# A conditioned residual block on one core: VectorE's last two lags of the convolution by quarters, the second pair of sums inside the variance's wait, short products of constants on TensorE, and the second spread one tile later

## The reference, cut to what matters

```
x = x + conv(x, cond)          # depthwise, causal: at position t, channel c the sum over lags j = 0..31
                               # of cond[31 - j, c] * x[b, t - j, c], nothing from before the sequence
ada = cond @ ada_w + ada_b     # shift1, scale1, gate1, shift2, scale2, gate2, one row for each sequence
x1 = ln(x) * (1 + scale1) + shift1      # ln: (x - mean) * (var + 1e-6) ** -0.5 over the 256 channels
q, k, v = split(x1 @ qkv_w + qkv_b)     # 16 heads of 128
y = x + gate1 * (softmax(q k^T / sqrt(128)) v @ out_w + out_b)
x2 = ln(y) * (1 + scale2) + shift2
y = y + gate2 * (gelu(x2 @ ffn_w1 + ffn_b1) @ ffn_w2 + ffn_b2)
out = x + y                    # x here with the convolution in it
```

## Time and profile before

| | |
|---|---|
| median of three runs | 312.05 us (311.78 to 312.29) |
| profiled execution, its own time | 311.19 us |
| span of its instructions | 309.4 us |
| granted TensorE clock over the span | 1.0 of full speed (2.4 GHz) |
| TensorE busy | 300.4 us (97%) |
| VectorE busy | 179.6 us (58%) |
| ScalarE busy | 174.6 us (56%) |
| GpSimd busy | 119.7 us (39%) |

### The profile page before, as it was taken

The page is one execution under the profiler, slowest core; times in us unless marked ns, Lnnn a source line. Parts: engine busy times, 40 slices in busy tenths (PEclk is TensorE's granted clock), DMA queues, the critical chain, the costliest instruction groups (busy, mean ns, idle before and its releaser), DMA issues.

```text
span 309.4 us, 6184 instructions
## 1 busy us (share of the span) xinstructions
PE 300.4 (97%) x2614; PEld 253.6 (82%) x2614; DVE 179.6 (58%) x311; ACT 174.6 (56%) x317; POOL 119.7 (39%) x104
## 2 busy tenths in 40 slices
PE   7989899999999999989999999999999999999995
PEld 7876797888898888878888888888898888878885
DVE  3996697987866648471446674350720455757232
ACT  5943368434762755466367636644763693824901
POOL 5215818331911543163327134630915471311500
PEclk9999999999999999999999999999999999999999
DMA  7902421500160061007002400520090000000022
GB/s 240 376 5 69 125 81 46 162 0 2 41 232 0 4 218 55 0 4 271 1 4 102 169 2 2 174 100 0 14 330 0 2 0 3 0 1 2 0 68 68
DMA packets 15275, 23.00 MB, mean 74 GB/s; under 512 B 808, under 2 KB 8336, under 8 KB 15248
## 3 DMA queue, kind: packets, MB, share of 16 engines
q1 hardware_dynamic: 15200, 22.58, 21.7%
q10 hardware_dynamic: 48, 0.03, 0.0%
HBM read 21.57 MB, written 1.05 MB: 73 GB/s over the span
## 4 chain that ended last, share of the span: by engine, by line
PE 86%; DVE 8%; POOL 2%; ACT 2%; issue 1%; DVEq 0%; POOLq 0%
PE bank L1025 16%; PE bank L1027 16%; PE bank L1026 16%; PE bank L1112 9%; DVE xc L592 5%; PE bank L1033 5%; PE bank L1034 4%; PE bank L1035 4%; PE bank L1096 3%; PE bank L1235 2%; PE bank L1237 2%; PE bank L1236 2%; POOL wl L309 1%; PE bank L964 1%; PE bank L1004 1%
## 5 line engine op out<-in xcount | busy, mean ns | idle before, releaser
L309 POOL TENSOR_TENSOR wl<-raw,wh 128x512 fp32r<-128x512 f32 x70 | 94.3, 1373 | 123.2 <-ACT wh L382 105.3
L433 ACT ACTIVATE pool<-bank,bT 128x512 f32<-128x512 f32 x56 | 38.5, 687 | 52.6 <-PE bank L1027 52.6
L1025 PE MATMUL bank<-x1h,wl 128*128 128x512 f32 (+1 forms) x174 | 65.7, 377 | 0.1
L1026 PE MATMUL bank<-x1l,wh 128*128 128x512 f32 (+1 forms) x174 | 64.6, 371 | 0.0
L1027 PE MATMUL bank<-x1h,wh 128*128 128x512 f32 (+1 forms) x174 | 64.6, 371 | 0.0
L732 DVE SCALAR_TENSOR_TENSOR ol<-bank,bT,oh 128x512 fp32r<-128x512 f32 x32 | 24.0, 750 | 34.0 <-ACT oh L458 33.0
L592 DVE SCALAR_TENSOR_TENSOR xc<-x,condT,xc 128x496 f32<-128x496 f32 (+27 forms) x80 | 42.1, 598 | 0.1
L382 ACT ACTIVATE wh<-raw 128x512 fp32r<-128x512 f32 x70 | 39.8, 622 | 0.0
L1025 PEld LDWEIGHTS bank<-x1h,wl 128*128 128x128 f32 x174 | 32.8, 189 | 6.3 <-POOL wl L309 0.5
L1027 PEld LDWEIGHTS bank<-x1h,wh 128*128 128x128 f32 x174 | 32.8, 188 | 5.7
L1026 PEld LDWEIGHTS bank<-x1l,wh 128*128 128x128 f32 x174 | 32.8, 188 | 5.3
(11 more groups left out here) (146 smaller groups left out, 433.4 us busy)
## 6 DMA issues: line engine op xcount, KB each, us to landing
raw<-in_L_cond_qkv_w_dram SPq DMA_DIRECT2D x24, 512.0 KB, 5.3
raw<-in_L_cond_out_w_dram SPq DMA_DIRECT2D x8, 512.0 KB, 3.6
raw<-in_L_cond_ffn_w_dram SPq DMA_DIRECT2D x3, 512.0 KB, 6.1
adaw<-in_L_cond_ada_w_dram SPq DMA_DIRECT2D x1, 1024.0 KB, 9.8
out_dram<-pool SPq DMA_DIRECT2D x3, 256.0 KB, 2.2
xtok<-in_x_dram SPq DMA_DIRECT2D x2, 256.0 KB, 3.2
adaw<-in_L_cond_ada_w_dram SPq DMA_DIRECT2D x1, 512.0 KB, 4.7
xtok<-in_x_dram SPq DMA_DIRECT2D x1, 512.0 KB, 5.7
```

The costliest lines, as they stand in the source:

```text
L309: g.tensor_tensor(wl[:, cols], raw[:, cols], wh[:, cols].bitcast(F32), ALU.subtract)\
L433: a.activation((q_sb if j < GH else k_sb)[:, j % GH, :], src, ACT.Identity, bias=bias(U, j // GH, j % GH)).then_inc(s_ev, 1)
L1025: pe.matmul(dst, wl[:, w_cols], a_hi, start=start, stop=False)
L1026: pe.matmul(dst, wh[:, w_cols], a_lo, start=False, stop=False)
```

## The change

There are four edits, all in the first 36 us.

1. VectorE's lags 11 and 12 of the first half (`END_LAGS`) are taken out of `conv(0, ...)` and made by quarters in a new function `conv_end(n)`, each with half the elements and twice as many instructions; `conv_sum(n)` waits for the end of `conv_end(n)` through a semaphore of its own.
2. The order on VectorE becomes: `conv_end(0)`, `conv_sum(0)`, `conv_end(1)`, `modulation(0)`, `centre(0)`, `one_plus`, `scale_up(0)`, `var_eps(0)`, and only then `conv_sum(1)`.
3. TensorE makes eight products of constants (32 columns of weights, 64 columns moving, into a bank that nobody reads then) before `mean(0)`.
4. `spread(1)` on TensorE stands behind tile 2 of the first quarter's projections instead of behind tile 1.

```diff
+    END_LAGS = DVE_LAGS[0][-2:]
+    STEPS_BEFORE = [0, CT * (len(DVE_LAGS[0]) - len(END_LAGS))]
...
+            def conv_end(n):
+                for i, j in enumerate(END_LAGS):
+                    for ct in range(CT):
+                        xs = by_batch(part(x0, ct, CHUNKS[n]))
+                        acc = by_batch(part(xc, ct, CHUNKS[n]))[:, :, j:]
+                        if i:
+                            v.wait_ge(s_cend[n], CT * (i - 1) + ct + 1)
+                        else:
+                            v.wait_ge(s_cdve, STEPS_BEFORE[1] - CT + ct + 1)
+                        v.scalar_tensor_tensor(out=acc, in0=xs[:, :, :T - j], scalar=condT[:, ct, T - 1 - j:T - j],
+                                               in1=acc, op0=ALU.mult, op1=ALU.add).then_inc(s_cend[n], 1)
+
             def conv_sum(n):
-                v.wait_ge(s_cdve, STEPS_BEFORE[1])
+                v.wait_ge(s_cend[n], CT * len(END_LAGS))
...
-            conv(0, 0, len(DVE_LAGS[0]))
+            conv(0, 0, len(DVE_LAGS[0]) - len(END_LAGS))
+            conv_end(0)
             conv_sum(0)
-            conv_sum(1)
+            conv_end(1)
             v.wait_ge(s_btc, 1)
             modulation(0)
+            centre(0)
             one_plus(0, SCALE1)
-            centre(0)
             scale_up(0)
             var_eps(0)
+            conv_sum(1)
             norm(0)
...
+            def short_idle_products(count):
+
+                for _ in range(count):
+                    pe.matmul(PB[1][0:T, 0:P // 2], ident[:, 0:T], ones[:, 0:P // 2], start=True, stop=True)
...
             conv(0, 16, len(PE_LAGS[0]))
+            short_idle_products(8)
             mean(0)
...
-            project_chunk(0, (1,))
+            project_chunk(0, (1, 2))
             spread(1)
-            project_chunk(0, (2, 3, 4, 5))
+            project_chunk(0, (3, 4, 5))
```

More of the change, by code:

```diff
@@ L68, in cond_resid_block_kernel @@
     BY_POOL = [(d, 1) for d in range(0, len(DIAG_LAGS), 2)]
-    STEPS_BEFORE = [0, CT * len(DVE_LAGS[0])]
+    END_LAGS = DVE_LAGS[0][-2:]
+    STEPS_BEFORE = [0, CT * (len(DVE_LAGS[0]) - len(END_LAGS))]
     with ExitStack() as ctx:
@@ L147, in cond_resid_block_kernel @@
         s_cfirst = sem("conv_first_lag_first_quarter")
+        s_cend = [sem("conv_end_first_quarter"), sem("conv_end_second_quarter")]
         s_adap, s_adac, s_adax = sem("ada_product"), sem("ada_rows_copied"), sem("ada_transposed")
```

## The result

The changed kernel took 312.26 us in the median of 17 runs (311.31 to 313.38), the kernel before 311.77 in 17 runs on the same chips (310.71 to 312.29). The ratio is 1.0027, 95% interval 1.0015 to 1.0040: slower by 0.3%. The forecast was 311.8, the same time within 0.2%; the measured time lies inside the stated range, but it moved, to the slower side and by more than the noise. The profiled execution of the changed kernel took 313.23 us (span 311.3), that of before 311.19 (309.4).

The account below looks back on a forecast made before the run. TensorE, busy 97%, was taken as the bound, started by the first normalization and held at unit 1 by GpSimd's low parts. Only 0.28 us was gained: 312.05 - 0.28 = 311.8 us, whole range 310.3 to 313.5.

Parts of the forecast that it names:

- part 3: New VectorE order in the first normalization: `centre(0)` at 22.95 for 23.62, gain 0.67, of which 0.29 is left at `var_eps`.
- the row at 47.40: Profile row before unit 1: GpSimd's low part took 2.97 us, waiting out VectorE's run; taken as model for 21.59.
- the gate at unit 1: Unit 1's projections wait for GpSimd's low parts, these for VectorE's run ending at 49.22; 51.68 stays but for 0.28.
- rival 2: GpSimd breaks into `conv_end(1)`: `centre(0)` at 25.1, 1.5 us later, total 313.6; chance 0.16.
- Part 1: Lags by quarters before the first sums: `conv_end(0)` takes 1.28 us, sums at 20.96 and 21.20, gain 0.68.
- Part 2: Constants' products before the first mean: sixteen passes take 0.9 us, mean starts at about 21.87, a loss of 0.2.
- The blocking of `scale_up`: In the first normalization GpSimd's second low part blocks `scale_up(0)` until 25.13, so `var_eps` starts at 25.67 for 25.96.
- the 0.28 forecast: Net gain from the first normalization, carried through quarter 1 to unit 1 and the total: 0.28 us.
- Part 4: Second spread behind tile 2: starts at 34.85, TensorE 1.02 us earlier after quarter 1's projections, lost at unit 1.
- Rival 1: At quarter 1 VectorE's `shift(1)` gets in before GpSimd's third low part: 1.26 us earlier, total 310.5; chance 0.20.
- rival 3: GpSimd breaks into VectorE's run at 46.1, before unit 1, delaying the softmax: total 313.0; chance 0.10.
- rival 4: Constants' products before the mean cost 0.11 a pass: `centre` at 23.9, 0.2 to 0.4 slower, 312.3; chance 0.06.

Follow-up runs that it names:

- experiments 7 and 8: 7: changed kernel, GpSimd's first low parts also wait for first quarter step, 312.69 us; 8: low parts not waiting for sums, kernel before 311.94, changed 311.02 us.
- experiment 5: Changed kernel plus three wide 128x512 products on TensorE before the first variance, collision left in: 311.18 us, ratio to the kernel before 1.0015.
- experiment 1: Kernel before with only the second spread moved behind tile 2: 310.58 us, ratio 0.9976.
- experiment 6: Kernel before with only the eight short products of constants before the first mean: 309.93 us, ratio 0.9956.
- experiment 3: Changed kernel, but GpSimd's first low parts also wait until quarter 1's quarter steps are done: 309.81 us, ratio to the kernel before 0.9955.
- experiment 9: Kernel of experiment 3 with two of VectorE's lags moved from before the first softmax to after it: 309.36 us, ratio to the kernel before 0.9943.
- experiment 4: Changed kernel plus ten 128x128 products on TensorE before the first variance, collision left in: 313.25 us, ratio to the kernel before 1.0082.

## Why the prediction was wrong, by its own steps

**The step that failed is in part 3**: "I take the row at 47.40 for it". The row was read rightly (GpSimd was kept out by a run, and the gate at unit 1 stands as predicted), but it was carried to a place unlike it. At 47.40 the run was eight steps old; after the sums of quarter 0 it is new, and there GpSimd gets in at the end of the first step (experiments 7 and 8). So rival 2 happened, with 0.16 the third likeliest: 3.30 us for the quarter steps, `centre` at 24.84 where it said 25.1. Its own price, 1.5 us, measured 1.3 at unit 1 (experiment 5). The Trainium skill (SBUF — State Buffer, Who interferes with whom) says that whoever issues first has the shared ports for the whole instruction. Read as the prediction reads it, that the one who waits comes in at that instruction's end, it gave the right answer at this place (21.58, let in at once) and the wrong one inside long runs (46.54, let in at about 49.1); neither it nor the row alone is the behaviour.

**The term that was missing is TensorE's clock.** The prediction said the clock was 1.0 all the way and priced nothing on it. The wait that rival 2 makes, 2.36 us, brought it down to 1.2 GHz, worth 0.6 to 1.1 us in the median (experiment 5 and the changed kernel). And the one profile of before hid that the clock also fell in half of its later runs. The sum took the 0.86 us between that profile and the median of three runs as a constant; those three runs, 311.78 to 312.29, lie in the group that goes with a fallen clock. So edits 4 and 3, held to be neutral or small, are worth 0.9 and 1.8 us in the median when alone: edit 4 by the clock (experiment 1), edit 3 by the clock and by the stall that it removes (experiment 6). That is also why rival 2 came out at 312.3 and not at 313.6. At full clock the changed kernel took 311.31, the faster group of before 310.7 to 311.0: the collision of 1.3 less the stall of 0.6 to 1.0; the fall of the clock then adds about 0.9 to both medians. That these add up to a time inside the range is luck: neither the clock nor the stall was in the sum.

**Part 1** held: 1.28, sums at 20.96 and 21.19. **Part 2** had its term too dear: no loss of 0.2; passes of 32 columns of weights and 64 moving start 0.056 apart, TensorE was free at 21.60, before the sums. The forecast's 0.67 at `centre` was 0.61 in experiment 3 and 0.81 in experiment 9, where it stood at 22.81. **The blocking of `scale_up`** held (`var_eps` 25.87 for a forecast of 25.67 in experiment 3), so of the 0.28 forecast 0.1 was left at unit 1. **Part 4** held: spread at 34.93, TensorE 0.96 early at unit 1, low part 3.84 us, unit 1 unmoved at 51.67 (experiment 1). Rival 1 did not happen (`shift(1)` took 1.85 after the change, where the rival had 1.2, and 2.26 in experiments 1 and 3); rival 3 fell (experiments 1 and 3: GpSimd asked in the eighth of twelve steps and was kept out through the last); rival 4 fell.

**The stall** at 133.5 stood in the profile of before and in its chain as "issue"; it was not in the sum. With 32 instructions more it was gone (experiment 6), with 40 more on top another came at 77.7 (experiment 4), so it can be a term of an edit that changes the number of TensorE's instructions.

## What to carry to other kernels

Before steps of VectorE with two SBUF operands are put behind a semaphore that also releases GpSimd, ask how many steps VectorE will have made when GpSimd asks: here a long unbroken run kept GpSimd out to its end and so gated whatever waits for GpSimd, and a fresh one was broken at once, at a whole GpSimd instruction (1.3 us) each. Read the granted clock of all timed runs, not only of the profiled one: an idle microsecond of TensorE decided here whether the clock fell, and cheap products in it were worth more than the quarter steps. Where an experiment adds TensorE instructions, search its trace for new "issue" stalls before its time is read.

## What the runs showed of the hardware

- GpSimd's 128x512 subtraction and VectorE's two-operand steps exclude each other. Asked in the first or second step of a run: served at that step's end (3.30 us for four steps of 1.28). Asked in the eighth step of a run or later: kept out for 1.7 to 2.9 us, to the run's end, also where that end is made of short steps (2.97, 3.19, 3.84, 4.18 for 1.27).
- TensorE's granted clock fell from 2.4 to 1.2 GHz 2.0 us into 2.36 us without a product, for 6.8 us; with 2.74 us of meaningless products there it stayed. In the kernel before, with idle times of 1.20 and 1.13 us, it fell in 31 of 62 runs; with the first cut to 0.55 it fell in none of 6, with the second filled in none of 12. With both gone it still fell in one of 6 in each of experiments 3 and 9, where no profile shows the place.
- TensorE stalled 1.0 or 1.6 us with nothing to wait for, at 133.5 or 77.7 us, and 32 instructions more removed the one, 40 more brought the other.
